# ScalarE normalises all four tiles of a block, and a block's first expert piece is joined, split and stored at the opening of the next block

## What is computed

```
x = x + gate(n) * y(n)          n = layernorm(x)
    s    = sigmoid(silu(n @ s_w1.T + s_b1) @ s_w2.T + s_b2)      128 states
    u    = (n @ B_w.T + B_b) * s
    h_t  = h_(t-1) @ A.T + u_t                                   a scan over the 4096 steps
    y    = h @ C_w.T + C_b + n @ D_w.T + D_b
    gate = sigmoid(n @ g_w.T + g_b)
x = x + m @ expert_w[e].T       m = layernorm(x),  e = argmax(m @ gate_w.T), one of 8 experts
```

## Time and profile before

| | us |
|---|---|
| median of 3 runs | 911.41 (909.81 to 911.87) |
| the profiled execution | 910.55 |
| its span, first to last instruction | 908.8 |
| PE busy | 890.0 (98%) |
| DVE busy | 685.2 (75%) |
| ACT busy | 635.7 (70%) |
| POOL busy | 428.5 (47%) |

### The profile page before, as it was taken

How to read it: one execution, slowest core, us unless ns; L and a number is a source line. 1 busy time by engine, 2 the same in 40 slices (tenths; PEclk the granted TensorE clock), 3 DMA queues, 4 the chain that set the end, 5 groups by cost and what they waited for, 6 DMA issues and landing times.

```text
span 908.8 us, 15716 instructions
## 1 busy us (share of the span) xinstructions
PE 890.0 (98%) x4413; PEld 719.9 (79%) x4414; DVE 685.2 (75%) x1697; ACT 635.7 (70%) x880; POOL 428.5 (47%) x671
## 2 busy tenths in 40 slices
PE   8999999999999999999999999999999999999996
PEld 7777878787887878787787878787878887888884
DVE  6777888888888878888787878888787465555552
ACT  5568687978878787978778787978534446666661
POOL 1134546282836546282826446282614454433442
PEclk9999999999999999999999999999999999999998
DMA  8436395858668495857778495856989979998871
GB/s 316 134 93 149 86 218 129 204 141 198 148 169 196 106 221 123 195 148 199 153 170 188 113 214 121 201 146 160 288 284 400 389 232 266 219 221 220 196 184 49
DMA packets 231051, 172.37 MB, mean 190 GB/s; under 512 B 155702, under 2 KB 189238, under 8 KB 229953
## 3 DMA queue, kind: packets, MB, share of 16 engines
q1 hardware_dynamic: 220032, 137.71, 61.3%
q0 software_dynamic: 10800, 33.70, 11.0%
q10 hardware_dynamic: 144, 0.07, 0.0%
HBM read 81.63 MB, written 54.68 MB: 150 GB/s over the span
## 4 chain that ended last, share of the span: by engine, by line
PE 84%; DVE 7%; issue 2%; DMA 1%; SPq 1%; ACT 1%; POOLq 0%; DVEq 0%; ACTq 0%
PE y L1774 19%; PE gates L1476 6%; PE y L1476 6%; PE y L1478 6%; PE y L1477 6%; PE gates L1477 6%; PE gates L1478 6%; PE turned L1661 3%; PE gates L1661 3%; PE scan L1620 3%; PE scan L1476 2%; PE scan L1478 2%; PE scan L1477 2%; PE turned L1763 2%; PE gates L1665 1%
## 5 line engine op out<-in xcount | busy, mean ns | idle before, releaser
L1774 PE MATMUL y<-experts,x1T_hi 128*128 x568 | 180.5, 399 | 0.0
L666 POOL DMA_INDIRECT out<-gate,ids x71 | 73.0, 1028 | 107.3 <-DVE gate L1441 67.2
L602 POOL TENSOR_SCALAR ln_var_eps<-ln_mean_var 128x4 f32<-128x4 f32 x16 | 3.7, 232 | 253.2 <-DVE ln_mean_var L1097 253.2
L1774 PEld LDWEIGHTS y<-experts,x1T_hi 128*128 128x128 f32 x568 | 103.2, 188 | 19.9 <-issue 0.2
L1774 PE MATMUL y<-experts,x1T_lo 128*128 x284 | 111.4, 392 | 0.0
L1476 PE MATMUL gates<-GwT_hi,xT_hi 128*128 128x512 f32 x256 | 104.7, 409 | 1.4
L592 POOL TENSOR_TENSOR y_biased<-y_biased,gate 128x256 f32<-128x256 f32 x120 | 94.0, 806 | 23.9 <-DVE y_biased L1087 23.9
L1476 PE MATMUL y<-DwT_hi,xT_hi 128*128 128x512 f32 x256 | 102.6, 401 | 0.5 <-DVE gateT L1019 0.5
L1441 DVE TENSOR_TENSOR gate<-y,raw_weights 128x512 f32<-128x512 f32 x71 | 49.1, 691 | 68.6 <-PE y L1774 42.6
L1477 PE MATMUL gates<-GwT_lo,xT_hi 128*128 128x512 f32 x256 | 100.6, 393 | 0.0
L1478 PE MATMUL gates<-GwT_hi,xT_lo 128*128 128x512 f32 x256 | 100.6, 393 | 0.0
(11 more groups left out here) (285 smaller groups left out, 2337.5 us busy)
## 6 DMA issues: line engine op xcount, KB each, us to landing
raw_weights<-routed_rows SPq DMA_DIRECT2D x71, 258.0 KB
x_in<-L_attn_x SPq DMA_DIRECT2D x32, 512.0 KB, 4.2
x_rows<-L_attn_x SPq DMA_DIRECT2D x32, 512.0 KB, 4.7
turned_experts<-raw_weights SPq DMA_DIRECT2D x32, 512.0 KB, 3.5
experts<-turned_experts SPq DMA_DIRECT2D x8, 2048.0 KB
raw_weights<-L_ffn_expert_w SPq DMA_DIRECT2D x32, 256.0 KB, 3.1
routed_rows<-padrow SPq DMA_DIRECT2D x9, 258.0 KB
out<-gate,ids POOLq DMA_INDIRECT x71
```

Of the source, the lines that this page charges most:

```text
L666: nc.gpsimd.indirect_dma_start(out=out_rows, out_offset=bass.IndirectOffsetOnAxis(ap=ids[r][:, 0:1], axis=0), in_=res[r], in_offset=None, ...
L1774: ins = nc.tensor.matmul(Y[m % 2][:], x2T[a][:, k, m % 2 * P:(m % 2 + 1) * P], flat[:, bass.ds(first + (w * KD + k) * D, D)], start=(k == ...
```

## The change

`normalise_late` is removed from POOL: `halve(b, i)` on ACT now normalises each of the four tiles itself. The semaphore `xn_late` goes with it. `join_piece` and `low_piece` of piece 0 move from the middle of `body(b)` to the opening of `body(b + 1)`: on ACT between `high` of the last tile and `halve_piece`, on DVE just ahead of `low_piece` of piece 1. SP issues both stores of a block one behind the other after the flips and loads of the next pieces, where it issued one there and one at the end of the body.

```
@@ sync
-                    if b == 1:
-                        store_piece(0, 0)
-                    store_piece(b - 1, 1)
+                    for j in range(2):
+                        store_piece(b - 1, j)
...
-                if 0 < b < LASTB:
-                    store_piece(b, 0)
-                elif b == 0:
+                if b == 0:
@@ gpsimd, rstd1
-                if b > 0:
-                    pool.wait_ge(S_["xn_ready"], NT + NT // 2 * (b - 1))
-                    wait(pool, S_["xn_late"], NT // 2 * (b - 1))
+                wait(pool, S_["xn_ready"], NT * b)
@@ gpsimd, body
-                if b < LASTB:
-                    normalise_late(b + 1, 2)
-                    normalise_late(b + 1, 3)
@@ scalar, halve
+                normalise1(b, i)
                 n = turn_of(b, i)
-                if i < NT // 2:
-                    normalise1(b, i)
-                    act.wait_ge(S_["xn_ready"], NT + NT // 2 * (b - 1) + i + 1)
-                else:
-                    act.wait_ge(S_["xn_late"], NT // 2 * (b - 2) + i + 1)
+                act.wait_ge(S_["xn_ready"], NT * b + i + 1)
@@ scalar, body
                     high(b, NT - 1)
                     if b > 1:
+                        join_piece(b - 1, 0)
                         halve_piece(b, 0)
...
-                if tail and ahead:
-                    join_piece(b, 0)
@@ vector, body
-                if b == 1:
-                    low_piece(0, 0)
                 if tail:
+                    low_piece(b - 1, 0)
                     low_piece(b - 1, 1)
...
-                if tail and ahead and not dma:
-                    low_piece(b, 0)
...
                     place(old, oldq, oldturn)
-                    if dma:
-                        low_piece(b, 0)
-                    else:
+                    if not dma:
                         ln2_stats(old, oldq, 3)
```

More of the change, by code:

```diff
@@ L186, in preln_ssm_moe_kernel @@
                      "bias_sum w_turned w_hi w_lo pow_psum pow_copied pow_hi pow_lo "
-                     "gate_stats gate_mean gate_centred stats1 mv1_ready ve1_ready rstd1_ready neg1_ready shift1_ready xn_ready xn_late xT_psum x_halves joined xT_hi xT_lo "
+                     "gate_stats gate_mean gate_centred stats1 mv1_ready ve1_ready rstd1_ready neg1_ready shift1_ready xn_ready xT_psum x_halves joined xT_hi xT_lo "
                      "s1_psum s1_sig silu_ready silu_hi silu_lo bt_psum s2_psum sel_ready "
@@ L627, in add_identity @@
                 nc.gpsimd.tensor_tensor(part, part, ident[:], ALU.add).then_inc(w_ident[j], 1)
[L629 to L633, removed]
             def body(b, q):
```

## The result

The changed kernel takes 922.62 us (median of 4 runs, 921.45 to 924.08) against 911.29 (4 runs, 909.81 to 911.87) before: ratio 1.0115, 95% interval 1.0099 to 1.0131. That is 11.3 us slower, where the prediction said 914.8 (its sum was +3.8) and 908.5 to 921.5 for the range. The direction was right and the size was not. The profiled execution took 921.45 us.

The account below looks back on a forecast made before the run. It took PE, busy 98% of the span, as the bound. Blocks 2 to 14 at -0.7 + 0.1 + 0.5 + 0.3 us each (+2.6), block 1 +0.8 and block 15 +0.4 gave +3.8: 914.8 us, range 908.5 to 921.5.

Parts of the forecast that it names:

- Released by POOL's normalisations, 0.7 us a block: Scan, blocks 2 to 14: without POOL's two normalisations DVE is on time and PE's stop goes, 0.7 us a block.
- L1228 held, 0.5 us a block (0 to 0.8): Block opening: POOL's late `residual` holds DVE's 2-element-wide addition, delaying PE's scan product; 0.5 us a block lost.
- s1 late by 0.3 us a block: Block end: tile 3's normalisation on ACT delays `xT_hi`, so PE waits 0.2 us plus 0.1 for the restart.
- Block 1, +0.8: Block 1: tile 2's normalisation goes in front of ACT's planes, for whose product PE waits already; +0.8 us.
- Block 15, +0.4: Block 15: no normalisation to lose but the second low part; +0.4 us.
- The sum without the DMA, +3.8: Whole kernel: +2.6 us over blocks 2 to 14, +0.8 in block 1, +0.4 in block 15, expert stage untouched.
- Hidden, with 0.4 us to spare: Second store ahead of the transpositions: 2.1 us more, join at about 210.4, covered by ACT's 1.52 us idle time.
- this as a rival: Stores delay transpositions by more than 2.5 us, ACT reaches the second `scoresT` late: 921 to 927 us, chance 0.17.
- The first rival: Scan opening: POOL's `residual` ends at most 0.1 us later, the 0.5 us is not lost: 907 us, chance 0.13.
- the terms cancel: New losses are 0.6 instead of 0.8 us a block, time within 0.2% of before: 910 to 913 us, chance 0.22.

Follow-up runs that it names:

- e6: The kernel before with nobody normalising tiles 2 and 3 of blocks 1 to 15: 904.13 us, ratio 0.9916.
- e5: e1 with the low part of piece 0 back at its old, late place on DVE in blocks 2 to 14: 912.23 us, ratio 1.0006.
- e1: The changed kernel with the store of piece 0 back at the end of SP's body in blocks 2 to 14: 916.26 us, ratio 1.0042.
- e2: The kernel before with only the normalisations moved to ACT, the expert piece staying in mid-block: 915.77 us, ratio 1.0046.
- e10: The changed kernel with both stores of blocks 2 to 14 between the transpositions of x1 and those of the tiles: 950.44 us, ratio 1.0424.
- e9: The changed kernel with both stores of blocks 2 to 14 at the end of SP's body: 915.65 us, ratio 1.0054.

## Why the prediction missed

Step by step, as the prediction had them:

- *Released by POOL's normalisations, 0.7 us a block.* Right: the whole gap at the scan's third product is gone. In the length of a block e6 puts it at 0.56, against 0.7 less 0.1 in the sum.
- *L1228 held, 0.5 us a block (0 to 0.8).* Right in kind in blocks 3 to 15, not in block 2. The size is 0.3 (0.20 late and 0.11 for the product behind it; e5 gives 0.3). PE stood at 240.61 in block 5, 14.80 us after s1; the forecast's 198.65 was 14.89 after.
- *s1 late by 0.3 us a block.* Right, 0.38. The account closes: e6's 40.46 with 0.31 and 0.38 added is 41.15, and a block of the changed kernel that no transposition delays takes 41.1 to 41.2.
- *Block 1, +0.8.* Right: 42.94 us instead of 42.17. *Block 15, +0.4:* too small: from its s1 to the first slot of the experts it takes 44.39 us instead of 43.28, +1.1. Where the rest comes from is open.
- *The sum without the DMA, +3.8.* Right in the blocks: the undisturbed ones of the changed kernel are 0.1 longer (0.2 forecast). That e1's medians give +4.0 is partly luck. In e1's profile blocks 2 to 14 are 2.2 us longer than before (2.6 forecast) and block 1 0.8, but block 15 is 1.4 longer (0.4 forecast) and the expert stage 1.3 (none forecast).
- *"Hidden, with 0.4 us to spare".* **This is the step that failed.** It priced a store as 512 KB at 246 GB/s, 2.1 us, and had the join at 210.4, which is 26.6 us after s1, with an edge at 27.0. Measured, the join starts 25.3 to 28.4 us after s1, against a landing at some 24.5 before. In the blocks where it starts at 27.2 or later (2, 6, 7, 8, 9, 12, 14) the block is long, in the six where it starts at 26.5 or earlier it is short. So the edge was placed well, and so was the mean: over blocks 2 to 14 the landing moved from 24.7 to 26.9 us after s1, 2.2 us. What was wrong is that one block's landing and a mean rate were taken for every block. The landings spread over 2.5 us before and over 3.2 after, with 0.4 us of room. The seven long blocks lose 7.1 us against before; with +0.7 in the short ones, +0.8 in block 1 and +1.1 in block 15 that is 9.7 of the 10.9 by which the span grew. Most of the rest, 1.5 us, lies in the expert stage, which nothing here changed and which varied by as much between the experiments.

The prediction had this as a rival, at 921 to 927 us with a chance of 0.17, and its test (ACT waiting for `flipped`, no idle time before the second `scoresT`) is what the profile shows. What should have raised the chance was in the profile before: its landings reach from 23.4 to 25.9 us after s1, and the one of the earlier trace rows, at 24.5, is below their mean. With 2.1 us on top, blocks 7, 9, 12 and 14 (25.5 to 25.9) pass the edge at 27.0 by 0.6 to 1.0 us each, an estimate of 3.2 us in all, where the prediction had none. Measured it was 7.1, in seven blocks, because the delay differs from block to block as well.

The first rival (the lock goes, nothing in its place) is refuted by the 478 ns, that the terms cancel by e1, whose interval (1.0025 to 1.0059) lies above no change. On the lock, the Trainium skill (SBUF — State Buffer, Who interferes with whom) says that issue order decides which of the two blocks; e2's two rows agree, 0.65 against 0.29 us with 0.4 us of difference in phase. The same section has it, as inferred, that an addition of two SBUF tiles and POOL's descriptor generation don't get in each other's way. The rows of e2 speak against it: the addition is stopped until POOL's indirect DMA is over. But POOL also reads the row numbers for this DMA from a tile in SBUF (`dest`), and no run tells the reading from the making of descriptors.

Two more things stay open. Why the same two stores delay a transposition by 1 us in one block and 4 in the next: the full DMA, the other transfers in flight and the order within them aren't separated here. And why the product's signal came late in blocks of e2.

## What to carry to other kernels

A transfer that is moved ahead of a latency-bound one on the same queue costs unevenly, and can cost more than its bytes divided by the bandwidth: 512 KB more, some 6 us ahead, made the landing 2.2 us later in the mean, as the rate gives, but 1 MB directly ahead made it 6.5 us later (e10 against e9), where 246 GB/s gives 4.3. Judge it by the latest landing in the trace, not by the mean, and put stores behind whatever somebody waits for. Work that collides with an engine can cost as much after being moved to another one (8.1 us on POOL, 9.9 on ACT): leave it out in an experiment on both sides before moving it. 0.4 us of room is none if the landing varies by 3.

## What the hardware showed that I had not expected

- Two 512 KB stores directly ahead of a transposition of 256 KB bring its time from issue to landing to 10.4 us in the block shown, and the whole kernel to +4.2%. The same two stores at the end of the body leave it at +0.5%, where the change's place gives +1.2%.
- A wait by a 2-element-wide DVE addition is paid in full: 0.32 us longer on DVE, 0.31 us a block on PE, some 4 us over the kernel.
- DVE's additions are held by POOL's indirect DMAs as well as by its arithmetic, and a difference of 0.4 us in phase switches it on or off (e2: 0.65 us in block 4, 0.29 in block 5).
- The event of a product's semaphore can stand up to 1.28 us behind the product's start where 0.29 us is usual (e2, blocks 3, 4, 6 and 10), and the blocks in which it does are the long ones.
